# A three-pass attention with gated output: two-head slots, loads by head group and an output projection on 128-token tiles

## The reference, cut to what matters

```
q = rms_norm((layernorm(x) @ Wq) split in 16 heads of 128)     # 16 x 112 tokens
k, v = from the context, 4 groups of 128, each shared by 4 heads
out = softmax(q k^T / sqrt(128)) v                             # 16 heads, 375 keys
x = x + tanh(g) * (out @ Wo)                                   # Wo: 2048 x 512
x = x + tanh(g') * attention2(layernorm(x))                    # 16 heads of 32, 112 keys, Wa, Wp
```

## Time and profile before

| | |
|---|---|
| median of 3 runs | 2170.64 us (2167.98 to 2171.20) |
| profiled execution, own time | 2167.37 us |
| its span, first to last instruction | 2165.7 us |
| mean granted TensorE clock | 0.973 |
| PE / DVE / ACT / POOL busy | 94% / 61% / 53% / 31% |
| stage of the second attention | about 1310 to 1847 us |
| last stage | about 1847 to 2166 us |

### The profile page before, as it was taken

One profiled execution on the slowest core, in us unless ns is written; L12 is line 12 of the kernel. 1 busy time (PEld: TensorE's weight loads), 2 busy tenths in 40 slices (PEclk: granted clock), 3 DMA queues, 4 the chain that ended last, 5 costly groups with the idle time before them and its releaser, 6 DMA issues. The chain is left out here.

```text
span 2165.7 us, 38580 instructions
## 1 busy us (share of the span) xinstructions
PE 2038.1 (94%) x13464; PEld 1689.3 (78%) x13464; DVE 1327.5 (61%) x2603; ACT 1140.9 (53%) x3025; POOL 666.6 (31%) x814
## 2 busy tenths in 40 slices
PE   6999999999989999999969995999999999689996
PEld 4777777777768888888848884888888888578884
DVE  6767767676634543663355555777777776366664
ACT  4666666666633333443334445667667665255453
POOL 2424435335221000000014443555555454012221
PEclk9999999999999999999979997999999999799997
DMA  5535445444284210100033343322322320311010
GB/s 154 155 97 172 126 133 191 126 146 136 85 259 140 78 39 1 68 30 1 1 126 120 119 125 124 109 91 71 108 99 67 104 99 13 117 43 44 30 32 27
DMA packets 167398, 205.96 MB, mean 95 GB/s; under 512 B 63680, under 2 KB 105664, under 8 KB 166752
## 3 DMA queue, kind: packets, MB, share of 16 engines
q1 hardware_dynamic: 167264, 204.15, 29.7%
HBM read 128.13 MB, written 75.99 MB: 94 GB/s over the span
## 5 line engine op out<-in xcount | busy, mean ns | idle before, releaser
L1729 POOL TENSOR_TENSOR c_probs<-c_probs,c_rsum 112x375 f32<-112x375 f32 x256 | 213.1, 835 | 231.3 <-DVE c_rsum L1839 225.5
L1835 DVE TENSOR_REDUCE c_nmax<-c_score 112x1 f32<-112x375 f32 x256 | 136.6, 535 | 97.8 <-PE c_score L1905 97.8
L1783 ACT ACTIVATE c_pT_hi<-c_turned 125x336 fp32r<-125x336 f32 x256 | 115.6, 452 | 108.2 <-PE c_turned L1913 108.2
L1224 ACT ACTIVATE b_silu<-b_gate,b_ug_scale 128x512 f32<-128x512 f32 (+1 forms) x64 | 40.7, 636 | 249.8 <-PE b_up L1330 249.8
L1281 DVE SCALAR_TENSOR_TENSOR b_hidden<-b_up,b_ug_scale,b_silu 128x512 f32<-128x512 f32 (+1 forms) x64 | 43.7, 683 | 203.5 <-ACT b_silu L1224 203.5
L1776 ACT ACTIVATE c_probs<-c_score,c_nmax 112x375 f32<-112x375 f32 x256 | 148.2, 579 | 0.0
L547 ACT ACTIVATE a_probs<-a_score,a_nmax 112x375 f32<-112x375 f32 x256 | 144.8, 577 | 4.6 <-DVE a_nmax L707 4.5
L1454 POOL TENSOR_TENSOR q_x_ve<-q_x_mv,keep_ln_eps 128x1 f32<-128x1 f32 x14 | 2.7, 191 | 444.8 <-DVE q_x_mv L1531 444.8
L918 PEld LDWEIGHTS a_turned<-keep_ident,a_probs 112*125 112x125 f32 x768 | 110.3, 188 | 34.3 <-issue 21.9
L2108 POOL TENSOR_TENSOR f_probs<-f_probs,f_rsum 112x448 f32<-112x448 f32 x64 | 60.3, 942 | 244.0 <-DVE f_rsum L2228 243.9
L2140 ACT ACTIVATE f_probs<-f_score,f_nmax 112x112 f32<-112x112 f32 x256 | 87.3, 354 | 90.9 <-DVE f_nmax L2223 90.2
(11 more groups left out here) (306 smaller groups left out, 5916.5 us busy)
## 6 DMA issues: line engine op xcount, KB each, us to landing
q<-q_qT SPq DMA_DIRECT2D x14, 1024.0 KB
c_q_raw<-q SPq DMA_DIRECT2D x16, 896.0 KB
k<-ab_stage SPq DMA_DIRECT2D x16, 752.0 KB, 4.5
c_k_raw<-k SPq DMA_DIRECT2D x16, 752.0 KB
v<-ab_stage SPq DMA_DIRECT2D x48, 250.0 KB
c_v_raw<-v SPq DMA_DIRECT2D x16, 750.0 KB
ab_lead<-in_ctx_dram SPq DMA_DIRECT2D x16, 672.0 KB
wug<-a_ug_turned SPq DMA_DIRECT2D x32, 256.0 KB, 2.4
```

The costliest lines, as they stand in the source:

```text
L1729: pool.tensor_tensor(probs[:, h % AHEAD, :], probs[:, h % AHEAD, :], rsum[:, p, h:h + 1].broadcast_to([S, T]), ALU.mult).then_inc(scaled, 1)
L1783: act.activation(pT[0][:, g % 2, :, j, :], src, ACT.Copy).then_inc(pT_hi, 1)
L1835: dve.tensor_reduce(nmax[:, p, h:h + 1], score[h % AHEAD][0:S, 0:T], axis=AX.X, op=ALU.max, negate=True).then_inc(max_done, 1)
```

## The change

In `phase_c_attention`:

- The loops go; all 256 heads are written out in one list of slots of two heads (`SLOTS` = 128).
- PE in slot u: `turn(2u)`, `turn(2u+1)`, `scores(2u+4)`, `scores(2u+5)`, then in odd slots `weigh((u-3)/2)`, in even slots `project((u-4)/2)`.
- q, k, v are loaded by head group (64 groups) into two raw buffers and split into rings of four. ACT and DVE split k in even slots and q (ACT also v) in odd slots.
- The output is collected in `oT` as columns by token (a ring of 256 tokens), and `project` works on tiles of 128 tokens over batch borders: 14 tiles instead of 16 batches. A group is projected only where the batch completes a tile (`tile_of`): batches 0 and 8 have no `project`. Where a batch crosses the ring's end (2, 4, 6, 9, 11, 13), `out_hi` and `out_lo` are two instructions (`pieces`).
- `finish` works on tiles; statistics, deviation (POOL) and normalization follow on each tile, and the normalized tokens are stored to a new tensor `xn3`.

In `phase_d`: `load_normal` reads `xn3` and `normalize` goes; the weights of `v` are split after item `k3` and not before it; the tokens of the second run are loaded before the weights `p`; `p` is split in two halves, in slots 0 and 1; the last run's `v1`, `v2`, `v3` move to slots 9, 11, 13 of that run (before: 8, 9, 9).

The core of the diff (SP and POOL as far as the text speaks of them; whole lines left out are marked):

```diff
+    def tile_of(b):
+        n = (b + 1) * S // P
+        return n - 1 if n > b * S // P else None
+    def finished(u):
+        t, odd = divmod(u - 4, 2)
+        b, g = divmod(t, G)
+        return tile_of(b) if u >= 4 and not odd and g == G - 1 and b < B else None
 ...
         def _(sp):
+            def load(t):
+                b, g = divmod(t, G)
+                r = t % RAW
+                if t >= RAW:
+                    sp.wait_ge(k_split, t - RAW + 1)
+                sp.dma_start(k_raw[:, r, :], io["k1"][b, :, g, :]).then_inc(k_loaded[r], 16)
+                if t >= RAW:
+                    sp.wait_ge(q_split, t - RAW + 1)
+                sp.dma_start(q_raw[:, r, :, :], io["q1"][:, HPG * g:HPG * g + HPG, b * S:(b + 1) * S]).then_inc(q_loaded[r], 16)
+                if t >= RAW:
+                    sp.wait_ge(v_split, t - RAW + 1)
+                sp.dma_start(v_raw[:, r, :, :], io["v1"][b, :, :, g * P:(g + 1) * P]).then_inc(v_loaded[r], 16)
+            def store(i):
+                sp.wait_ge(x_done, i + 1)
+                sp.dma_start(by_tiles(io["x3"])[i, :, :], xout[:, i % 2, :]).then_inc(x_stored[i % 2], 16)
+                sp.wait_ge(n_done, i + 1)
+                sp.dma_start(by_tiles(io["xn3"])[i, :, :], xnorm[:, i % 2, :]).then_inc(n_stored[i % 2], 16)
 ...
         def _(act):
+            def out_hi(t):
+                b, g = divmod(t, G)
+                act.wait_ge(out_ready, t + 1)
 ...
+                for tokens, place in pieces(b):
+                    last = act.activation(oT[0][:, HPG * g:HPG * g + HPG, place], src[:, :, tokens], ACT.Copy)
+                last.then_inc(o_hi, 1)
+            keys_hi(0)
+            queries_hi(0)
+            keys_hi(1)
+            queries_hi(1)
+            values_hi(0)
+            for n in range(AHEAD):
+                exps(n)
+                if n == 1:
+                    values_hi(1)
+            for u in range(SLOTS + 3):
+                if u % 2 == 0 and u >= 4:
+                    out_hi((u - 4) // 2)
+                for n in (2 * u, 2 * u + 1):
+                    if n < HEADS:
+                        probs_hi(n)
+                for n in (2 * u + AHEAD, 2 * u + AHEAD + 1):
+                    if n < HEADS:
+                        exps(n)
+                t = u // 2 + 2
+                if t < GROUPS:
+                    if u % 2 == 0:
+                        keys_hi(t)
+                    else:
+                        queries_hi(t)
+                        values_hi(t)
 ...
         def _(dve):
+            for n in range(AHEAD):
+                maximum(n)
+                reciprocal(n)
+            for u in range(SLOTS + 8):
+                if u % 2 == 0 and 4 <= u < SLOTS + 3:
+                    out_lo((u - 4) // 2)
+                for n in (2 * u, 2 * u + 1):
+                    if n < HEADS:
+                        probs_lo(n)
+                    if n + AHEAD < HEADS:
+                        maximum(n + AHEAD)
+                i = finished(u - 1)
+                if i is not None:
+                    finish(i)
+                for n in (2 * u + AHEAD, 2 * u + AHEAD + 1):
+                    if n < HEADS:
+                        reciprocal(n)
+                t = u // 2 + 2
+                if t < GROUPS:
+                    if u % 2 == 0:
+                        keys_lo(t)
+                    else:
+                        queries_lo(t)
+                i = finished(u - 2)
+                if i is not None:
+                    moments(i)
+                i = finished(u - 4)
+                if i is not None:
+                    normalize(i)
 ...
         def _(pe):
+            def project(t):
+                b, g = divmod(t, G)
+                i = tile_of(b)
+                if i is None:
+                    return
+                pe.wait_ge(o_split, t + 1)
 ...
+                place = slice(i * P % TOKENS, i * P % TOKENS + P)
+                for n, (s, r) in enumerate(PASSES):
+                    for j in range(HPG):
+                        last = pe.matmul(y[:, :], oT[s][:, HPG * g + j, place], wo[r][:, HPG * g + j, :],
 ...
+            for n in range(AHEAD):
+                scores(n)
+            for u in range(SLOTS + 3):
+                for n in (2 * u, 2 * u + 1):
+                    if n < HEADS:
+                        turn(n)
+                for n in (2 * u + AHEAD, 2 * u + AHEAD + 1):
+                    if n < HEADS:
+                        scores(n)
+                if u % 2 and u >= 3:
+                    weigh((u - 3) // 2)
+                if u % 2 == 0 and u >= 4:
+                    project((u - 4) // 2)
 ...
 def phase_d(nc, keep, io):
+    LAST = {2: "q0", 3: "k0 q1", 4: "k1", 5: "q2 k2", 6: "q3", 7: "k3 v0", 9: "v1", 11: "v2", 13: "v3"}
+    WP_PARTS = 2
 ...
-            for name in weights:
+            for name in weights[:-1]:
                 load_weight(name)
+            for b in range(BPG, 2 * BPG):
+                load_normal(b)
+            load_weight("p")
             for b in range(2):
                 load_residual(b)
-            for b in range(BPG, 3 * BPG):
+            for b in range(2 * BPG, 3 * BPG):
                 load_normal(b)
 ...
             item_hi(0, "q3")
+            item_hi(0, "k3")
             weights_hi("v")
-            item_hi(0, "k3")
 ...
-                if u == 0:
-                    weights_hi("p")
+                if u < WP_PARTS:
+                    output_weights_hi(u)
```

More of the change, by code:

```diff
@@ L41 @@
 RMS_EPS = 1e-6
-NORM_EARLY = B - 2
 PASSES = ((0, 0), (0, 1), (1, 0))
@@ L1684, in phase_c_attention, with by_tiles @@
         block = m.block()
[L1686 to L1691, removed]
+        def by_tiles(tensor):
+            return tensor.rearrange("b s d -> (b s) d").rearrange("(t p) d -> t p d", p=P)
         @block.sync
         def _(sp):
[L1695 to L1699, removed]
[L1701 to L1723 removed]
@@ L1861, in body @@
-            def body(before, cur, after):
-                norm_early(norm_moments, dve, keep, norm, cur)
-                def ahead(what, n):
-                    if n < H:
-                        what(cur[0], cur[1], n)
-                    elif after:
-                        what(after[0], after[1], n - H)
-                if cur and not before:
-                    for h in range(AHEAD):
-                        maximum(cur[0], cur[1], h)
-                    for h in range(RECIPROCAL):
-                        reciprocal(cur[0], cur[1], h)
-                for h in range(H):
-                    done = group(SPLIT_OUT, h, before, cur)
-                    if done:
-                        out_lo(*done)
-                    if cur:
-                        ahead(reciprocal, h + RECIPROCAL)
-                        ahead(maximum, h + AHEAD)
-                        probs_lo(cur[0], h)
-                    if h == FINISH and before:
-                        finish(*before)
-                    if h in SPLIT_K and after:
-                        keys_lo(after[0], after[1], SPLIT_K[h])
-                    if h in SPLIT_Q and after:
-                        queries_lo(after[0], after[1], SPLIT_Q[h])
@@ L1939, in body @@
-            def body(before, cur, after):
-                if cur and not before:
-                    for h in range(AHEAD):
-                        scores(cur[0], cur[1], h)
-                for h in range(H):
-                    if cur:
-                        turn(cur[0], h)
-                    if cur and h + AHEAD < H:
-                        scores(cur[0], cur[1], h + AHEAD)
-                    elif after and h + AHEAD >= H:
-                        scores(after[0], after[1], h + AHEAD - H)
-                    done = group(WEIGH, h, before, cur)
-                    if done:
-                        weigh(*done)
-                    done = group(PROJECT, h, before, cur)
-                    if done:
-                        project(*done)
@@ L2246, in finish @@
                                          op0=ALU.mult, op1=ALU.add).then_inc(x_done, 1)
-            for b in range(BPG):
-                normalize(b)
             weights_lo("q0")
```

409 lines of the change are left out of this document (192 added, 217 removed).

## The result

The kernel after takes 2225.33 us (median of 4 runs, 2224.78 to 2226.66), the kernel before 2170.86 beside it (2167.98 to 2171.2): a ratio of 1.0255, 95% interval 1.0237 to 1.0273. It is **slower by 54.5 us**. The prediction had the sign, but 2186 is 39 us too low and the range ended at 2210.

What follows compares the result with a forecast made beforehand. PE's list was taken to bound the attention, at 7.95 us per group. On the profiled 2167.4 us, 33.3 - 3 + 2.4 - 9 - 4 - 1 = +18.7 gave 2186 us, range 2148 to 2210.

Steps and rivals of the forecast that it cites:

- part 2: Attention, new order in a slot: the 22.4 us of saved projections shrink to 0.7, and the attention's sum is +33.3 us.
- The walk: Timing of one pair of attention slots, step by step: PE stands 0.45 us at `project` for `out_lo`, 8.40 us per group.
- the walk's floor: Attention: the other engines' lists need about 7.86 us per group even without `project`, where PE alone would need 5.15.
- Part 1: Attention batches 0 and 8 lose 4 `project` each: 22.4 us of PE, the gain if PE still sets the pace.
- Stationary columns, loops, loads: Attention: 128 stationary columns in `project` keep 2.80 us, written-out loops gain nothing, smaller loads cost nothing.
- The start: Start of the attention: loads by group bring the first `exps` to 1320.6 and head 8 to 1339: -3 us (0 to -8).
- Between the stages: Last `finish` to next load: 7.0 us in place of 4.1, 0.5 back for normalization: +2.4 us (0 to +5).
- The last stage: Two PE waits (4.70, 6.03 us) go, `p` is late next: -9 us; moved items -4, normalizations leaving DVE -1.
- The second: Rival: no PE stall in the attention, since ACT reaches `out_hi` in time: 2152 us; chance 0.26.
- the third: Rival: neither stall nor floor, attention batches 0 and 8 run at PE's 5.15 us: another 21.7 off, 2131; chance 0.04.
- The fourth: Rival: the clock falls to 1.2 GHz in the attention batches without `project`: +20 us, 2206; chance 0.07.
- The fifth: Rival: attention loads queue behind `store`'s wait for `normalize`, `keys_hi` waits in each of 14 tiles: +28 us, 2214; chance 0.07.

Runs made afterwards that it cites:

- run two: Kernel after, with GpSimd scaling only the first column of each head's probabilities: 2193.98 us, ratio 1.0118 to the kernel before.
- run three: Kernel after, with queries split one head group earlier and GpSimd scaling one column only: 2188.0 us, ratio 1.0082 to the kernel before.
- the last experiment: Kernel after, with key and query splits moved into gaps of the same slot and `values_hi` moved behind `out_hi`: 2148.3 us, ratio 0.99 to the kernel before.
- the kernel in head order: Kernel after, attention one head at a time as in the kernel before: 2222.34 us; with `values_lo` later 2191.49; with deviation and normalization later too 2150.62.

## Why the prediction was right or wrong

**The step that failed** is part 2, in two places: its line on the even slot, "two turns, two scores, `project` wanted at 5.15", and the length of two subtractions on VectorE.

- *A wait left out.* The walk let the even slot's `scores` start behind the turns. They are the first of a new group and wait for `q_split`, which `queries_lo` of the odd slot just before gives. The walk had the number that should have stopped it: `queries_hi` at 3.45 puts `queries_lo` at 4.03, and the walk's turns are over at 4.0. With 0.63 us for it, scores come at about 4.7 and the period at 8.62 to 8.66; run two showed 8.62. The wait for `out_lo`, on which the prediction had spent its care, lies inside this one.
- *A duration from another neighbourhood.* From the earlier trace rows `queries_lo` was taken at 0.55 from start to next start (its row is 0.63 long), and the walk's floor gave `keys_lo` 0.46. In the new order both stand right behind the reciprocals that release POOL's scalings, and take 1.07 and 1.05. The first costs 0.45 us in each group with a projection (9.07 against 8.62), both together 0.64 in each without (8.47 against 7.83). The Trainium skill, "SBUF — State Buffer", section "SBUF: two separate sides", says this outright: VectorE with two SBUF inputs and GpSimd take a shared pair of ports as an exclusive lock, and the other fully blocks. The trace agrees, with 1035 against 625 ns for `queries_lo`. By that rule the 1.64 us of scalings ahead of `queries_lo` belonged in the walk.

The rest, by the prediction's own steps:

- **The walk itself** held. Time 0 is 1510.37, and the two engines' rows give the second maximum at 2.29 (walk 2.30), the second exponential at 2.87 (2.90), `queries_hi` at 3.43 (3.45), `values_hi` at 3.90 (3.92) and `out_hi` at 4.31 (4.35):

```profile
1512.66 0.54 DVE L1832 TENSOR_REDUCE c_nmax<-c_score 112x1 f32<-112x375 f32 x1
```
```profile
1513.24 0.57 ACT L1771 ACTIVATE c_probs<-c_score,c_nmax 112x375 f32<-112x375 f32 x1 [0.20 <-DVE c_nmax L1832]
...
1513.80 0.57 ACT L1752 ACTIVATE c_q_hi<-c_q_raw 128x448 fp32r<-128x448 f32 x1
1514.27 0.51 ACT L1764 ACTIVATE c_v_hi<-c_v_raw 125x384 fp32r<-125x384 f32 x1
1514.68 0.59 ACT L1790 ACTIVATE c_oT_hi<-c_outp 128x256 fp32r<-128x256 f32 x2
```

  No row stands between `queries_hi`, `values_hi` and `out_hi`, as forecast. And run three shows that its stall and its sum were right for a kernel without the two faults. The size came out at 18.6 for 18.7; that close a match is partly luck, since the pieces and the statistics cost less (0.12 for 0.17 and 0.18 for 0.4) and the period more (8.45 for 8.40).
- **Part 1** was right that the saved projections would shrink to nothing: the batches without them are bound by the lists, at 8.47 us and more here. In the last experiment they do pay, at 6.65 us a group.
- **Stationary columns, loops, loads** at nothing: right, by the 7.97 to 8.02 us of the kernel in head order. Behind the start of the attention no engine waits for a load in it.
- **The start**: first `exps` at 1321.36, forecast 1320.6; the ninth head's transposes at 1340.67 for 1339, so 1.3 us won and not 3. Here too the scores of a new group had stood for their queries, 2.08 us ahead of 1334.58.
- **Between the stages**: 6.29 us from the last `finish` to the next load (1912.35 to 1918.64) for the 7.0 estimated, +1.6 in all for +2.4.
- **The last stage**: -13.3 for -14. Of the two waits of the earlier trace rows, the scores wait once for `k3`, 1.2 us where it was 4.70, and the transposes at most 0.8 at a time where it was 6.03; ACT waits for `p` only 0.6 us, once. Next late was `v`:

```profile
1958.57 1.67 PE L2348 MATMUL f_work<-f_w_hi,f_xT_hi 128*112 128x512 f32 x4 [1.72 <-DVE f_w_lo L2218]
```

  In the last 45 us of each span PE works 34.85 us where it worked 30.55, at a granted clock of 0.84 where it was 0.75. That fits the forecast of 4 us for the moved items, though no kernel moved them alone.
- **The rivals.** The second (no stall, 2152) falls, and so does the third: no group of batches 0 and 8 is under 8.47 us. The fourth is the clock. It is granted at 0.90 in batch 8 from 1655 to 1672 (second line of the first fence on busy time), where PE is busy for 79%; but the two groups in that stretch take 8.48 and 8.47 us, as most of batch 0, so the lists set the period there. It costs in two other groups. The one behind batch 0, with the first projection, takes 10.61 us, 1.5 over the others; the two lines below stand at its start. And the second group of batch 8 takes 9.51, 1.0 over 8.47: from 1642.79 on its scores' matmuls start 0.31 us apart in place of 0.17.

```profile
1374.00:1378.00 4.00, 1.72 (x11) 1.36 (x11) 3.04 (x8) 3.32 (x9) 2.62 (x3) 1.00 0.18 48
1378.00:1383.00 5.00, 5.00 (x18) 4.06 (x16) 3.06 (x8) 1.73 (x5) 1.98 (x3) 0.66 0.35 86
```

  That is a mechanism with the right place and an eighth of the price (2.5 us, and 20 were forecast for it). In both groups TensorE had stood for 2.08 us just before; it had stood as long ahead of 1343.64 and of 1660.78, in groups that lost nothing. The fifth, a late SP, falls too: ACT waits for no load there.

The direction was right, the range was not: its upper end came from doubling the one stall that the walk had found, and no width around a found stall covers a wait that was not looked for.

## What to carry to other kernels

When the order of several engines' lists is rewritten, take every wait in the code of the bounding engine, one by one, and put the time of its releaser beside it, not only those of the wait that seems tightest. Then look at what GpSimd does beside each VectorE operation that takes two tensors, or here `normalize`'s one, from SBUF: the duration that you find for it in a trace belongs to the place where you found it. And where an engine's list has a gap ahead of a wait, work with no hurry belongs into the gap and not behind the wait: here moving the statements of three copies and two subtractions was worth 77 us out of 2225.

## What the runs showed that I had not expected

- VectorE's subtractions of two SBUF tensors took 0.55 and 0.62 us with GpSimd kept short, and 1.05 and 1.07 beside its scalings; GpSimd's 384-element subtraction took 1.0 to 1.04 us without VectorE's beside it and 1.39 with it. The lost time stands in the profile as a longer instruction and not as idle time before it. A subtraction with one operand in PSUM stayed at 0.50 in either case.
- Two losses overlapped: taking away the wait for the queries (17 us) and the blocking (31 us) gave 37 us together, not 48.
- On GpSimd, one operation that waits too early is enough: in head order it cost 31 us in `values_lo` and 41 in `deviations`, each by holding up the scalings behind it, though GpSimd is busy for little more than half of the stretch (258 of 495 us).
